# A mixture-of-experts layer's down product split in three, and ScalarE's order changed in the attention phases

## The chip, the core and the metric

The kernel runs on one core of a Trainium2 chip. The metric is the device time of one execution in microseconds (us). In the text PE is TensorE (its matmuls; PEld its weight loads), DVE is VectorE, ACT is ScalarE, POOL is GpSimd and SP is SyncE, which only issues DMAs here.

## The reference, cut to what matters

Sixteen sequences of 128 tokens with 128 features go through eight phases; each phase adds tanh(gate) times its result to x. Phases 0, 2, 4, 6 are attentions of different kinds, phases 1, 3, 5, 7 feed-forward layers. Phase 7 is the one that the change is mostly about, a mixture of 32 routed experts with hidden size 64, top 8 per token chosen within the best 4 of 8 groups, plus a shared expert of hidden size 128:

```
h    = layernorm(x)
s    = sigmoid(h @ router) (+ bias);  w = top-8 weights within the top 4 groups, normed, times 2.5
out  = sum_e w_e * ((silu(h @ Wg_e) * (h @ Wu_e)) @ Wd_e)  +  (silu(h @ Sg) * (h @ Su)) @ Sd
x    = x + tanh(g) * out
```

Every expert is computed for every token, and the weight w is zero for those not chosen.

## The kernel before

Tokens are held in four groups g of 512. A *step* is one group in one phase. Phase 0 comes first, then phases 1 and 3 (with phase 2 riding along) as `STREAMS[0]`, then phases 4 to 6 as *units* of attention heads (`heads_pe`, `heads_act`, `heads_dve`), then phase 7 as `STREAMS[1]`.

**A stream** (`stream_pe`, `stream_act`, `stream_pool`, `stream_dve`, lines 952 to 1282) goes through chunks n = 0, 1, ... In phase 7 each of the four groups has 17 chunks of 128 hidden rows (i = 0 is the shared expert, i = 1 to 16 routed ones), 68 in all. For one chunk:

- PE: the gate product into bank `B[n % 2]` and the up product into one of three banks, each as three fp32r matmuls of 128x512 (L870 to L872: high part of the weights by the low and the high part of x, low part of the weights by the high part of x). That is `product`.
- ACT: `sg = silu(gate)` (L1085), a ring of three.
- DVE: `hid = sg * up` (L1249), a ring of ten in SBUF.
- POOL, for i > 0: `hid *= bcs`, the token weights of this chunk's experts, spread over the partitions by DMA (L1213).
- PE, eight chunks later (`LAG`): the down product `Y += Wd * hid` as one fp32 matmul (L945, `stream_down`); a profile shows an fp32 matmul as two records.

Engines work in order, each through its own program. PE waits for `sg_ready` of chunk n-2 before a gate product, for `product_ready` of chunk n-3 before an up product, and for `weighted` before a down product. Hooks put steps of the next group at fixed chunks of the present one. In phase 7, for the next group: `xt` (transposes of its normed x, i = 1), `logits` (i = 4, in group 0 i = 6), `result` of the group before (i = 11), `turn` (i = 15, L969). `turn` transposes `comb`, the routing weights of the next group, waits for `comb_ready`, and stands in PE's program behind the products of chunk 15 and ahead of its down product. On ACT the sigmoid of the logits (`scores_act`, L905) comes one chunk after `logits` and needs another table: one table load before it and one before the next silu. On DVE the routing (`route_groups`) is a generator: from the chunk after `logits` on, one piece of it behind each product, seven pieces, the last one `comb` (L619). In group 0 these are chunks 7 to 13. The statistics of a later group (i = 10) and the update of x (L256, i = 11) stand among them. The transposed `comb` is copied to `w_row` by ACT (`turned_act`, chunk 16), stored and spread by SP's DMAs.

**The attention phases** work in units n of four heads by one sequence, 16 to a cycle c. PE's order in a unit: score(n), shift(n-1), the small steps of unit n (`compact_pe`, `rows`, `heads_turned_pe`, `result`, `values_pe`, `slots_pe`), turn(n-2), weigh(n-3). ACT's order in unit n: the small steps of unit n (L1470, L1361, L280, L287, and those of `slots_act`, L1957 and L1960 among them), exp of scores n (L1699), the copy `pt` of the transposed n-1 (L1709), the copy `os`. DVE takes the maxima (L1832) and its own small steps.

The lines quoted, from `stream_down`:

```python
nc.tensor.matmul(Y[:], w_raw[2][:, at:at + P], hid[(n0 + c) % HIDDEN],
                 start=(i == 0), stop=(i == m["NC"] - 1))
```

## Time and profile before

| what | value |
|---|---|
| median of 3 runs | 839.27 us (838.12 to 840.56) |
| the profiled execution | 840.37 us, span 838.6 us |
| phase 7 | about 670.9 us to the end |
| mean granted TensorE clock | 0.992 |

The span runs from the first to the last instruction; the execution's own time is 1.8 us longer. Rows give start, duration (us), engine, line, operation, output<-input, and in brackets the idle time of the engine before it with what ended it. Matmul records include their way through the array, so starts tell the spacing, not ends. The three matmul lines L870 to L872 are told from another by their tile names: gate or up.

### The profile page before, as it was taken

Reading aid. Unit: us, or ns where it says so; the run is one execution under the profiler, and the core shown is the slowest. Engines: PE = TensorE matmul, PEld = TensorE weight load, DVE = VectorE, ACT = ScalarE, POOL = GpSimd, SP = SyncE. Lnnn points to the kernel's source line nnn. Section 1 sums busy time; section 2 is a strip of 40 time slices with the busy share of each in tenths; the row PEclk is TensorE's granted clock in tenths of the full one; section 3 lists DMA queues with packets and bytes.
Section 4 is the critical chain, followed back from the end, with each engine's and each line's share of the span. In section 5 each row is a group of like instructions: output and inputs, shape, how many; then the busy total and the mean of one; then the engine's idle time right before and its main releaser. Section 6 shows DMA issues by size and latency. Waiting matters only on the chain.

```text
span 838.6 us, 13371 instructions
## 1 busy us (share of the span) xinstructions
PE 812.8 (97%) x4371; PEld 552.5 (66%) x4371; DVE 476.2 (57%) x1383; ACT 417.8 (50%) x762; POOL 446.2 (53%) x429
## 2 busy tenths in 40 slices
PE   4999999999999999999999999999999999999998
PEld 4876666777667666665666666656566576666664
DVE  6766536394846555335555757576755756545331
ACT  2434565656556343324666676756555562434221
POOL 5284655466654645376555444354545457565453
PEclk9799999999999999999999999999999999999999
DMA  9213030314423142441334131322213042424241
GB/s 317 83 50 102 1 101 1 100 65 159 134 70 100 53 145 57 139 123 41 80 95 114 42 98 44 97 49 54 64 41 90 28 150 69 148 71 145 70 154 46
DMA packets 44868, 75.27 MB, mean 90 GB/s; under 512 B 8992, under 2 KB 9632, under 8 KB 44672
## 3 DMA queue, kind: packets, MB, share of 16 engines
q1 hardware_dynamic: 44656, 74.42, 29.8%
q8 instruction: 35, 0.57, 0.3%
q14 instruction: 33, 0.27, 0.1%
q10 hardware_dynamic: 144, 0.01, 0.0%
HBM read 56.11 MB, written 1.51 MB: 69 GB/s over the span
## 4 chain that ended last, share of the span: by engine, by line
PE 87%; DVE 7%; ACT 2%; issue 2%; DMA 1%; SPq 0%; ACTq 0%; DVEq 0%
PE Y L945 21%; PE B L870 11%; PE B L872 11%; PE B L871 11%; PE B L1552 5%; PE B L1571 3%; PE B L1533 3%; PE B L1539 3%; PE B L1532 2%; PE T L1351 2%; DVE mxh L1832 2%; PE T L962 1%; DVE xhat L1815 1%; DMA CT<-in_ctx_t 1%; PE Y L1475 1%
## 5 line engine op out<-in xcount | busy, mean ns | idle before, releaser
L1213 POOL TENSOR_TENSOR shared<-shared,bcs 128x512 f32<-128x512 f32 x192 | 247.7, 1295 | 213.8 <-DVE shared L1249 189.4
L1249 DVE TENSOR_TENSOR shared<-shared,B 128x512 f32<-128x512 f32 x204 | 139.9, 687 | 222.5 <-PE B L872 182.9
L1085 ACT ACTIVATE shared<-B 128x512 f32<-128x512 f32 x204 | 121.7, 598 | 251.7 <-PE B L872 250.9
L945 PE MATMUL Y<-shared,down_lo 128*128 128x512 f32 x408 | 207.5, 594 | 0.0
L1772 POOL TENSOR_TENSOR shared_r<-shared_r,const 128x512 fp32r<-128x512 f32 (+1 forms) x128 | 115.6, 933 | 79.5 <-PE B L1533 37.4
L1832 DVE TENSOR_REDUCE mxh<-B 128x4 fp32r<-128x512 f32 (+1 forms) x128 | 78.7, 618 | 83.8 <-PE B L1533 82.7
L1709 ACT COPY shared<-B 128x512 f32<-128x512 f32 (+1 forms) x128 | 64.6, 505 | 59.8 <-PE B L1552 59.8
L1699 ACT ACTIVATE shared<-B 128x512 f32<-128x512 f32 (+1 forms) x128 | 69.4, 543 | 49.4 <-PE B L1539 47.9
L945 PEld LDWEIGHTS Y<-shared,down_lo 128*128 128x128 f32 x408 | 72.5, 190 | 21.4 <-issue 9.5
L870 PE MATMUL B<-shared_r,gate_hi 128*128 128x512 f32 x102 | 81.0, 795 | 0.0
L870 PE MATMUL B<-x_lo_r,gate_hi 128*128 128x512 f32 x102 | 75.7, 742 | 0.0
L1552 PE MATMUL B<-const,shared 128*128 128x128 f32 x448 | 71.9, 277 | 0.2 <-ACT shared L1709 0.2
L1552 PEld LDWEIGHTS B<-const,shared 128*128 128x128 f32 x448 | 53.6, 142 | 23.0 <-issue 14.2
L1533 PE MATMUL B<-shared_r 128*128 128x512 f32 (+1 forms) x128 | 67.2, 525 | 1.1 <-ACT shared L1699 1.1
L1539 PE MATMUL B<-mxh,minus_r 128*128 128x512 f32 (+1 forms) x128 | 48.3, 377 | 4.4 <-DVE mxh L1832 4.1
L1571 PE MATMUL B<-shared,vh 128*32 128x128 f32 x768 | 40.9, 285 | 0.0
L871 PE MATMUL B<-x_hi_r,gate_hi 128*128 128x512 f32 x102 | 40.6, 398 | 0.0
L872 PE MATMUL B<-shared_r,up_lo_r 128*128 128x512 f32 x102 | 40.5, 397 | 0.0
L872 PE MATMUL B<-x_hi_r,up_lo_r 128*128 128x512 f32 x102 | 40.4, 396 | 0.0
L872 PE MATMUL B<-x_hi_r,gate_lo_r 128*128 128x512 f32 x102 | 40.3, 395 | 0.0
L871 PE MATMUL B<-x_hi_r,up_hi 128*128 128x512 f32 x102 | 40.3, 395 | 0.0
L870 PE MATMUL B<-x_lo_r,up_hi 128*128 128x512 f32 x102 | 40.2, 394 | 0.0
(317 smaller groups left out, 1398.2 us busy)
## 6 DMA issues: line engine op xcount, KB each, us to landing
bcs<-wrow SPq DMA_DIRECT2D x96, 256.0 KB, 3.7
shared_r<-shared_r SPq DMA_DIRECT2D x256, 64.0 KB, 2.0
bcs<-wrow SPq DMA_DIRECT2D x128, 128.0 KB, 3.0
gate_lo<-in_moe SPq DMA_DIRECT2D x9, 256.0 KB, 5.3
up_lo<-in_moe SPq DMA_DIRECT2D x9, 256.0 KB, 6.0
down_lo<-in_moe SPq DMA_DIRECT2D x9, 256.0 KB, 3.7
small<-in_small SPq DMA_DIRECT2D x1, 1372.5 KB, 12.0
X<-in_x SPq DMA_DIRECT2D x4, 256.0 KB, 5.2
```

Of the source, the lines that this page charges most:

```text
L870: nc.tensor.matmul(out, w_hi[w][:, cols], lo, start=start, stop=False)
L871: nc.tensor.matmul(out, w_hi[w][:, cols], hi, start=False, stop=False)
L872: return nc.tensor.matmul(out, w_lo[w][:, cols], hi, start=False, stop=stop)
L945: nc.tensor.matmul(Y[:], w_raw[2][:, at:at + P], hid[(n0 + c) % HIDDEN], start=(i == 0), stop=(i == m["NC"] - 1))\
L1085: nc.scalar.activation(sg[(n0 + n) % ACTIVE], B[n % GATES][:], ACT.Silu).then_inc(sem("sg_ready"), 1)
L1213: gp.tensor_tensor(hid[(n0 + n) % HIDDEN], hid[(n0 + n) % HIDDEN], bcs[(PLACE.k0[p] + r // m["PER"]) % BROADCAST], ALU.mult)\
L1249: nc.vector.tensor_tensor(hid[(n0 + n) % HIDDEN], sg[(n0 + n) % ACTIVE], up[:], ALU.mult)\
L1533: mm(out, qh[a][:, cols], k_each[a % 2][:, :, cols], start=(p == 6), stop=True)\
L1539: mm(SC[u % 2][0:w, 0:4 * w].rearrange("p (i k) -> p i k", i=HEAD_TILES), minus_r[0:w, 0:w], mxh[u % 2][0:w, :].unsqueeze(2).to_broadcast( ...
L1552: ins = nc.tensor.transpose(PT[:, c], es[u % 2][:, c], ident)
L1772: ins = nc.gpsimd.tensor_tensor(k_each[a % 2][:, i, cols], kh[a % 2][:, cols].bitcast(F32), K("rowmask")[:, i:i + 1].to_broadcast([P, TG * ...
L1832: v.tensor_reduce(mxh[n % 2][0:w, :], SC[n % 2][0:w, 0:4 * w].rearrange("p (i k) -> p i k", i=4), AX.X, ALU.max).then_inc(sem("max_ready"), 1)
```

## The change

Chunks i = 5 to 16 of every group of phase 7 (`split`, 48 of them) get their down product as three fp32r matmuls instead of one fp32: high weights by low hid, high weights by high hid, low weights by high hid. For that:

- the down weights of these 12 chunks are split once: ACT copies the high part (`down_hi`) at chunks 3, 5, 7, four chunks of weights each, POOL subtracts for the low part at chunks 5, 7, 9;
- in a split chunk POOL multiplies `sg` by `bcs` ahead of DVE's product; DVE writes sg * up back into the up bank (PSUM); ACT copies it to `hid_hi` (`high`, in iteration n+1, after silu of n+1); DVE subtracts for the low part into `hid_low` (`low`, in iteration n+1, ahead of the product of n+1);
- phase 7's stream has four up banks instead of three, and the up product of chunk n+4 waits for `low` of n;
- the result copy of the group before moves from ahead of silu of chunk 8 to behind silu of chunk 7.

In `heads_act` the small steps of unit n+1 are issued between exp of n and the copy `pt` of n-1. Before, they came behind that copy. Of the `slots_act` steps only those at t = 1, 2 and 14 move, the others stay ahead of exp.

```diff
+WHOLE, HIGHS = 5, 10
+late = Area()
+down_hi = late.at_tile(15, [P, (MOE[7]["NC"] - WHOLE) * P], shared_r)
+hid_hi = [late.at_tile(18 + i, [P, TG], shared_r) for i in range(HIGHS)]
+def down_piece(q):
+    a, b = PIECES[7][q]
+    return slice((a - WHOLE) * P, (b - WHOLE) * P)
...
 bcs = [sb(f"bcs{i}", [P, TG])[:] for i in range(BROADCAST)]
+hid_at = area1.at
 hid = [area1.tile([P, TG]) for i in range(HIDDEN)]
+hid_low = [shared_r[:, hid_at + i * TG:hid_at + (i + 1) * TG] for i in range(HIDDEN)]
...
         self.n0 = PLACE.n0[phases[0]]
+        self.ups = UPS if ride else UPS + 1
+        self.split = {}
+        for n, (G, i) in enumerate(self.chunks):
+            p, g = self.groups[G]
+            if p == 7 and i >= WHOLE:
+                self.split[n] = len(self.split) + 1
...
+    def upper(self, n):
+        return B[GATES + n % self.ups]
...
             pe.wait_ge(sem(f"raw_down3_{q}"), 16)
+    if c in run.split:
+        for q, (a, _) in enumerate(PIECES[p]):
+            if (g, i) == (0, a):
+                pe.wait_ge(sem("down_lo_ready"), q)
+        at, w = i * P, (i - WHOLE) * P
+        hi, lo = hid_hi[run.split[c] % HIGHS], hid_low[(n0 + c) % HIDDEN]
+        pe.wait_ge(sem("hid_lo_ready"), run.split[c])
+        nc.tensor.matmul(Y[:], down_hi[:, w:w + P], lo, start=False, stop=False)
+        nc.tensor.matmul(Y[:], down_hi[:, w:w + P], hi, start=False, stop=False)
+        nc.tensor.matmul(Y[:], w_lo[2][:, at:at + P], hi, start=False, stop=(i == m["NC"] - 1))\
+            .then_inc(sem("down_mm") if i < m["NC"] - 1 else sem("y_ready"), 1)
+        return
...
                 .then_inc(sem("gated_mm"), 1)
-            if n >= UPS:
-                pe.wait_ge(sem("product_ready"), n0 + n - UPS + 1)
+            if n - run.ups in run.split:
+                pe.wait_ge(sem("hid_lo_ready"), run.split[n - run.ups])
+            elif n >= run.ups:
+                pe.wait_ge(sem("product_ready"), n0 + n - run.ups + 1)
...
                 pe.wait_ge(sem("p0_updated"), 2)
-            product(B[GATES + n % UPS][:], 1, slice(at, at + P), x_hi[g % 2], x_lo[g % 2])\
+            product(run.upper(n)[:], 1, slice(at, at + P), x_hi[g % 2], x_lo[g % 2])\
...
+    def high(n):
+        act.wait_ge(sem("product_ready"), n0 + n + 1)
+        k = run.split[n]
+        if k > HIGHS:
+            freed = next(c for c in run.split if run.split[c] == k - HIGHS)
+            H, i = run.chunks[freed]
+            after_down(act, *run.groups[H], i)
+        nc.scalar.copy(hid_hi[k % HIGHS], run.upper(n)[:]).then_inc(sem("hid_hi_ready"), 1)
...
         p, g = run.groups[G]
-        if i == LAG and G > 0:
+        if i == LAG and G > 0 and n - 2 not in run.split:
...
         nc.scalar.activation(sg[(n0 + n) % ACTIVE], B[n % GATES][:], ACT.Silu).then_inc(sem("sg_ready"), 1)
+        if G > 0 and i == LAG - 1 and n - 1 in run.split:
+            result_act(act, run.groups[G - 1][0], run.step(G) - 1)
+        if n - 1 in run.split:
+            high(n - 1)
+        if p == 7 and n in DOWN_ACT:
+            q = DOWN_ACT[n]
+            act.wait_ge(sem(f"raw1_{q}"), 96)
+            nc.scalar.copy(down_hi[:, down_piece(q)], w_raw[2][:, piece(7, q)])\
+                .then_inc(sem("down_hi_ready"), 1)
...
             weights_hi(act, 3, *SPLIT_ACT[n])
+    if len(run.chunks) - 1 in run.split:
+        high(len(run.chunks) - 1)
...
 SPLIT_ACT = {57: (0, 0), 58: (0, 1), 62: (1, 0), 63: (1, 1), 66: (2, 0), 67: (2, 1), 69: (3, 0), 70: (3, 1)}
+DOWN_ACT = {3: 1, 5: 2, 7: 3}
+DOWN_POOL = {5: 1, 7: 2, 9: 3}
...
             pool.wait_ge(loaded, count)
-            pool.wait_ge(sem("product_ready"), n0 + n + 1)
-            gp.tensor_tensor(hid[(n0 + n) % HIDDEN], hid[(n0 + n) % HIDDEN],
+            if n in run.split:
+                pool.wait_ge(sem("sg_ready"), n0 + n + 1)
+                by_weight = sg[(n0 + n) % ACTIVE]
+            else:
+                pool.wait_ge(sem("product_ready"), n0 + n + 1)
+                by_weight = hid[(n0 + n) % HIDDEN]
+            gp.tensor_tensor(by_weight, by_weight,
...
                 .then_inc(sem("weighted"), 1)
+        if p == 7 and n in DOWN_POOL:
+            q = DOWN_POOL[n]
+            c = piece(7, q)
+            pool.wait_ge(sem("down_hi_ready"), q)
+            gp.tensor_tensor(w_lo[2][:, c], w_raw[2][:, c], down_hi[:, down_piece(q)].bitcast(F32),
+                             ALU.subtract).then_inc(sem("down_lo_ready"), 1)
...
+    def low(n):
+        dve.wait_ge(sem("hid_hi_ready"), run.split[n])
+        if n >= HIDDEN:
+            H, i = run.chunks[n - HIDDEN]
+            after_down(dve, *run.groups[H], i)
+        nc.vector.tensor_tensor(hid_low[(n0 + n) % HIDDEN], run.upper(n)[:],
+                                hid_hi[run.split[n] % HIGHS].bitcast(F32), ALU.subtract)\
+            .then_inc(sem("hid_lo_ready"), 1)
...
             st.restart()
-        dve.wait_ge(sem("sg_ready"), n0 + n + 1)
-        dve.wait_ge(sem("upper_mm"), n0 + n + 1)
-        up = B[GATES + n % UPS]
-        if n >= HIDDEN:
-            before = run.chunks[n - HIDDEN]
-            after_down(dve, *run.groups[before[0]], before[1])
-        nc.vector.tensor_tensor(hid[(n0 + n) % HIDDEN], sg[(n0 + n) % ACTIVE], up[:], ALU.mult)\
-            .then_inc(sem("product_ready"), 1)
+        if n - 1 in run.split:
+            low(n - 1)
+        up = run.upper(n)
+        if n in run.split:
+            dve.wait_ge(sem("weighted"), PLACE.r0[p] + g * MOE[p]["NR"] + i - MOE[p]["SHARED"] + 1)
+            dve.wait_ge(sem("upper_mm"), n0 + n + 1)
+            nc.vector.tensor_tensor(up[:], sg[(n0 + n) % ACTIVE], up[:], ALU.mult)\
+                .then_inc(sem("product_ready"), 1)
+        else:
+            dve.wait_ge(sem("sg_ready"), n0 + n + 1)
+            dve.wait_ge(sem("upper_mm"), n0 + n + 1)
+            if n >= HIDDEN:
+                before = run.chunks[n - HIDDEN]
+                after_down(dve, *run.groups[before[0]], before[1])
+            nc.vector.tensor_tensor(hid[(n0 + n) % HIDDEN], sg[(n0 + n) % ACTIVE], up[:], ALU.mult)\
+                .then_inc(sem("product_ready"), 1)
...
             norm_stats(st, (run.step(H) + 2) % NG, run is STREAMS[0])
+    if len(run.chunks) - 1 in run.split:
+        low(len(run.chunks) - 1)
...
+OF_PE = (1, 2, 14)
 def heads_act(act):
-    for n in range(ALL + 3):
+    def step(n):
...
                 result_act(act, group(c - 1)[0], S4 + c - 1)
+            if t in OF_PE:
+                slots_act(act, c, t)
+    for n in range(ALL + 3):
+        c, t = divmod(n, NU)
+        if c < CYCLES and t not in OF_PE:
...
                                  scale=SCALEH).then_inc(sem("heads_es_ready"), 1)
+        step(n + 1)
```

## Rows read from the trace of the kernel before

**Rows 1.** The page, busy time, share of the span and instructions of each engine.

```profile
PE 812.8 (97%) x4371; PEld 552.5 (66%) x4371; DVE 476.2 (57%) x1383; ACT 417.8 (50%) x762; POOL 446.2 (53%) x429
```

**Rows 2.** The page, the chain that ended last, by line.

```profile
PE Y L945 21%; PE B L870 11%; PE B L872 11%; PE B L871 11%; PE B L1552 5%; PE B L1571 3%; PE B L1533 3%; PE B L1539 3%; PE B L1532 2%; PE T L1351 2%; DVE mxh L1832 2%; PE T L962 1%; DVE xhat L1815 1%; DMA CT<-in_ctx_t 1%; PE Y L1475 1%
```

**Rows 3.** The timeline of PE in group 0 of phase 7.

```profile
674.69 0.39 PE L871 MATMUL B<-x_hi_r,gate_hi 128*128 128x512 f32 x1
676.09 0.39 PE L871 MATMUL B<-x_hi_r,gate_hi 128*128 128x512 f32 x1
...
690.84 0.39 PE L871 MATMUL B<-x_hi_r,gate_hi 128*128 128x512 f32 x1
...
700.31 0.39 PE L871 MATMUL B<-x_hi_r,gate_hi 128*128 128x512 f32 x1
702.57 0.39 PE L871 MATMUL B<-x_hi_r,gate_hi 128*128 128x512 f32 x1
...
703.73 0.60 PE L969 MATMUL T<-const,comb 128*32 128x128 f32 x4
```

**Rows 4.** The timeline of ACT, chunks 7 and 8.

```profile
685.58 0.60 ACT L1085 ACTIVATE shared<-B 128x512 f32<-128x512 f32 x1 [1.03 <-PE B L872]
686.19 1.28 ACT L905 ACT_TABLE_LOAD   x1
...
687.78 1.28 ACT L1085 ACT_TABLE_LOAD   x1
689.08 1.09 ACT L1085 ACTIVATE shared<-B 128x512 f32<-128x512 f32 x2
```

**Rows 5.** The timeline of DVE, routing in group 0, and L688 of group 1.

```profile
689.76 0.69 DVE L1249 TENSOR_TENSOR shared<-shared,B 128x512 f32<-128x512 f32 x1 [0.20 <-ACT shared L1085]
690.36 0.38 DVE L593 MAX8 m<-gv 128x8 f32<-128x12 f32 x4
...
698.73 1.31 DVE L688 SCALAR_TENSOR_TENSOR w<-work,sig 128x128 f32<-128x128 f32 x1
...
701.42 0.28 DVE L619 SCALAR_TENSOR_TENSOR comb<-w,rec 128x128 f32<-128x128 f32 x1
...
734.22 0.90 DVE L688 SCALAR_TENSOR_TENSOR w<-work,sig 128x128 f32<-128x128 f32 x1
```

**Rows 6.** Busy us of PE, PEld, DVE, ACT, POOL; then clock, DMA share, GB/s.

```profile
689.76:701.70 11.94, 11.94 (x46) 8.11 (x45) 11.46 (x48) 3.40 (x6) 8.19 (x8) 1.00 0.30 89
```

**Rows 7.** Groups of instructions: xcount, busy us, mean ns, idle before.

```profile
L1268 DVE TENSOR_TENSOR shared_r<-T,shared_r 128x512 fp32r<-128x512 f32 x1 | 0.7, 691 | 0.1
L1103 ACT CAST shared_r<-T 128x512 fp32r<-128x512 f32 x6 | 3.6, 606 | 0.0
L1213 POOL TENSOR_TENSOR shared<-shared,bcs 128x512 f32<-128x512 f32 x192 | 247.7, 1295 | 213.8 <-DVE shared L1249 189.4 <-DMA bcs<-wrow 24.0
L2026 DVE TENSOR_TENSOR B<-B,m 128x256 f32<-128x256 f32 x4 | 1.7, 432 | 0.1
L2001 DVE TENSOR_TENSOR x_lo<-x_lo,B 128x256 f32<-128x256 f32 x4 | 1.7, 420 | 0.1
```

**Rows 8.** The timeline of POOL beside L688.

```profile
698.61 1.28 POOL L1213 TENSOR_TENSOR shared<-shared,bcs 128x512 f32<-128x512 f32 x1
```

**Rows 9.** Busy time in two stretches, columns as in rows 6 (PE, PEld, DVE, ACT, POOL, clock).

```profile
637.75:641.16 3.41, 2.06 (x15) 1.21 (x14) 2.73 (x4) 1.05 (x4) 3.41 (x4) 1.00 0.41 101
641.16:644.58 3.42, 3.42 (x15) 2.48 (x14) 1.03 (x2) 1.97 (x4) 0.31 (x1) 0.50 0.43 101
```

**Rows 10.** The timeline of DVE and PE in group 1: comb and turn.

```profile
737.93 0.28 DVE L619 SCALAR_TENSOR_TENSOR comb<-w,rec 128x128 f32<-128x128 f32 x1
744.15 0.60 PE L969 MATMUL T<-const,comb 128*32 128x128 f32 x4
```

**Rows 11.** Waits in the attention phases: waiting<-waited for, total us, times, longest.

```profile
PE B L1926 <- ACT bcs L1960: 0.4, 2, 0.3
PEld B L1926 <- ACT bcs L1960: 2.2, 4, 0.7
```

## The prediction

> **What bounds the kernel now.** I read the page first: TensorE (PE) is busy in 97% of the span, DVE in 57%, ACT in 50%, POOL in 53% [rows 1], and the chain that ended last lies mostly on PE, 21% of it on the down product, L945 [rows 2]. So I then read PE's own timeline in phase 7. A chunk without a down product takes 676.09 - 674.69 = 1.40 us from one L871 to the next; it is six fp32r matmuls, so 0.234 us each. A chunk with its fp32 down product takes 702.57 - 700.31 = 2.26 us [rows 3]. The fp32 product thus costs 0.86 us of PE. From chunk 8 on no PE row of phase 7 shows a wait: the stage is PE's issue time and nothing else. Last I read ACT and DVE in the same stretch, for how late they may become before PE waits [rows 4 to 6], and the list of waits in the attention phases for the reorder.
>
> **1. The split down product.** Removed: 48 fp32 products (4 groups, 12 of 17 chunks) at 0.86 us. Added: 3 fp32r matmuls each, of the form of L870 to L872, 3 x 0.234 = 0.70 us. PE saves 0.16 us per chunk at most; over all chunks the period with a down product is nearer to 2.25, so I take 0.15: 48 x 0.15 = 7.2 us (7.7 at 0.16). All of it is on the path, since PE is. The last eight down products are among the 48.
> The Trainium skill (TensorE: Matmul & The Clock Gate, Back-to-back issue gap) has N/2.4 + 2.5 ns, 216 ns for 512 columns; by that three products would cost 0.65 us and the split would save 10.3 us instead. The trace spaces these very matmuls at 0.234 us, so it disagrees, and the row is what I use.
>
> **2. What the split puts on the other engines.** Per split chunk, DVE gets the subtraction `low` (the form of L1268, 0.69 us; what follows such an op starts 0.60 after it, 690.36 behind 689.76), ACT gets the copy `high` (L1103, 0.61 us), POOL's multiplication stays at 1.29 us but is now ahead of DVE's product instead of behind it [rows 5, 7]. The product is now written to PSUM; for 128x256 the writes to PSUM (L2026, 0.432) and to SBUF (L2001, 0.420) cost the same [rows 7], so nothing is added. The way of one chunk becomes silu, weight, product, high, low: 0.60 + 1.29 + 0.69 + 0.61 + 0.69 = 3.9 us, about 4.4 with five hand-overs of 0.1 (silu's end at 689.68 to the product at 689.76 is 0.08 [rows 4, 5]). Down products come eight chunks later, and behind the very last chunk seven other down products and its own up product still cover 8 x 0.70 = 5.6 us, so the tail is not lengthened. The four up banks leave about 4 us of lateness: up product n+4 is wanted 4 x 2.1 = 8.4 us after n's gate, `low` of n is nominally done 4.2 us after it. On average all is covered: DVE adds 48 x 0.60 = 29 us and ACT about as much to engines half idle. It is not covered where routing stands.
>
> **3. ACT at chunk 7.** Before: silu of 7 at 685.58, sigmoid table 686.19, silu table 687.78, silu of 8 at 689.08 [rows 4]. In that same iteration ACT now also issues `high` of 6 and the last copy of down weights, 0.49 to 0.61 each: silu of 8 starts at 690.2 and ends at 690.8. PE wants its bank for chunk 10 at about 690.4 (its second matmul, L871, was at 690.84 [rows 3]). PE waits some 0.4 us; between 0 and 1. The other two weight copies (ACT, chunks 3 and 5) and the three subtractions on POOL (1.3 us each, chunks 5, 7, 9) are nominally within idle time: ACT is idle over 1 us per chunk, and POOL 0.9. If that cover were gone they would add to this same wait.
>
> **4. DVE's routing in group 0.** This is the step that decides. PE's `turn` for group 1 stands after chunk 15, at 703.73 [rows 3], and waits for comb. All later matmuls of PE are queued behind it. In the trace comb ends at 701.42 + 0.28 = 701.70 [rows 5], 2.0 us early. From the product of chunk 8 (689.76) to there DVE is busy 11.46 of 11.94 us [rows 6], with six products and routing, statistics and the update between them; the rest is starts. After: the product of 8 waits for silu (690.8), for POOL's 1.29 and two hand-overs: 692.4. Five `low` (8 to 12) go between, 5 x 0.60 = 3.0. Comb ends at 692.4 + 11.9 + 3.0 = 707.3. PE arrives two shortened down products earlier (-0.3) but 0.4 later by part 3: 703.8. So PE waits 3.5 us, 3.6 with the hand-over. Bounds: 2.5 (L688 at 0.90 as in group 1 instead of 1.31 [rows 5], and the product of 8 some 0.6 sooner) and 5 (0.69 for each `low` and product, and 0.5 of waiting for `high`).
> L688, one of the routing instructions, took 1.31 us here, with POOL's L1213 at work from 698.61 [rows 5, 8], and 0.90 in group 1; I keep 1.31. The Trainium skill (SBUF — State Buffer, Who interferes with whom) says that a DVE instruction with two SBUF inputs and a GpSimd instruction that reads SBUF block each other; L688 fits that, `low` and product have one PSUM input each and would stay at 0.69, and were the block gone by the new order the sum would be 0.4 us less.
>
> **5. The clock.** In the attention stage, from 637.75 to 641.16, PE was busy 2.06 of 3.41 us, so idle for 1.35; in the next stretch, 3.42 us, the granted clock was 0.50, the 1.2 GHz level [rows 9]. A full stop of 3.6 us at `turn` is longer than that one, and the matmuls before and behind it are the dense kind, which speaks a little against it. At half the clock 3.4 us yield the work of 1.7 us: a cost of 1.7, or 0. I take 1.7.
> That idle time lets the granted clock fall is also in the Trainium skill (TensorE: Matmul & The Clock Gate, Part 1); the trace agrees with its level.
>
> **6. Groups 1 and 2.** There routing begins two chunks earlier. In group 1 comb starts at 737.93 and `turn` at 744.15 [rows 10]: 6 us early. Seven `low` take 4.2, POOL's place ahead of the product up to 1.4 at the start, PE's own gain over ten chunks up to 1.0 the other way. Between 0 and 2 us remain, so I take no wait; group 3 routes nothing. Later there: w_row is copied on ACT behind `high`, one or two us later, so the first multiplications of a group begin later on POOL; its chunks 1 to 4 are not split and their down products are eight chunks away.
>
> **7. ACT's order in the attention phases.** Nothing is added. The small steps that PE issues ahead of the transposes of a unit (compact, rows, heads turned, result, three of the slot steps) are now taken by ACT in that order, not behind the copy of the unit before. Each is ready 0.5 to 1 us sooner; the transposed copy may come later but has a whole unit till it is used. What can be won are PE's waits for such steps: at L1926, the largest of them, the array was idle for 0.4 us and the weight load for 2.2 [rows 11]. The first is a floor, since much of a weight load's wait lies under the matmul before it, the second a ceiling. The other steps wait less, so I stay between: -1.2. Bound on the other side: +0.5, from the last cycle's short units, where a copy of 0.6 comes ahead of a pt copy.
>
> **The sum**, against the profiled execution (840.37 us, span 838.6 and 1.8 around it): -7.2 + 0.4 + 3.6 + 1.7 - 1.2 = -2.7, or 837.7. It was 1.1 above the median of the runs, 839.27; on that the forecast is 836.6 us.
>
> **Rivals.**
> *The wait at `turn` stays away or is small* (DVE absorbs `low`; product of 8 early). For: over the whole span DVE is busy 57% only. Against: the 11.94 us without idle time. Then -7.2 - 1.2 = 830.9. Chance 0.12.
> *The wait comes, the clock holds.* For: PE stood dense before and after. Then 836.6 - 1.7 = 834.9. Chance 0.25.
> *The forecast, wait and clock:* 836.6. Chance 0.40, half of it below and half above 836.75.
> *A longer wait, 5 to 6 us, with the clock:* 838 to 839. Chance 0.13.
> *Slower: DVE late at all three turns.* If x us more are lost between routing's start and comb in each group (two-input routing ops at 1.31 like L688, `low` waiting for ACT), the waits are 3.6 + x, x - 1 and x - 2 and two more clock falls at 1.7 follow. At x = 3 that is 3 x 3 + 0.6 = 9.6 and 5.1 for clocks, less 8.4 and with 0.4 from part 3: +6.7, 846. It turns slower than before at x = 2 (5.6 + 1.0 of waits, one or two falls at 1.7, against 8.0). For: DVE is full in that stretch. Against: the routing starts two chunks earlier there. Chance 0.10.
>
> **How the numbers follow.** A measurement tells 0.3%, 2.5 us, from no change, so the border is 836.75. Faster: 0.12 + 0.25 + about 0.15 = 0.52. Same: the rest of the forecast and 0.13, 0.38. Slower by over 2.5 us: 0.10. The range, 831.5 to 840.5, leaves out the last case and most of the first; its lower end is the saving nearly whole, its upper end is the longer wait with the reorder worth nothing.
>
> **What would show it.** Right: 144 fp32r matmuls at 0.23 us in phase 7 and chunks with them 2.10 us apart; one PE wait of 3 to 4 us ahead of the transposes of comb after chunk 15, released by DVE L619, none at the later two; a stretch at half clock behind it; DVE without idle time from the product of chunk 8 to comb. Wrong: no PE wait there (then 831), PE waiting for `low` ahead of an up product (banks too few), or split chunks over 2.2 us apart. In the attention phases, the wait before L1926 gone and no new one before L1571.

## The result and the profile after

The changed kernel takes 835.35 us (median of 4 runs, 833.73 to 835.43) against 839.91 us (4 runs, 838.12 to 840.56) of the kernel before, run beside it: ratio 0.9944, interval 0.9924 to 0.9965. The forecast was 836.6 us with a range of 831.5 to 840.5. The profiled execution after took 833.73 us, with a span of 831.9. It was the fastest of the four; the other three took 835.3 to 835.4 us at a mean granted clock of 0.989, against 0.993 here, so they spent more time at the lower clock. In the start-up of the kernel, ahead of all that was changed, it is 1.1 us ahead of the profiled execution before. The clock goes with that: from about 20 us on it was at the 1.2 GHz level for 10.2 us before and for 3.4 us after.

The page of the kernel after, first the engines, then the chain by line, then groups of instructions (busy us, mean ns | idle before, and its releaser):

```profile
PE 802.1 (96%) x4419; PEld 559.9 (67%) x4419; DVE 503.6 (61%) x1431; ACT 445.6 (54%) x813; POOL 450.6 (54%) x432
...
PE Y L979 15%; PE B L892 10%; PE B L894 10%; PE B L893 10%; PE B L1641 5%; PE B L1660 4%; PE B L1622 3%; PE B L1628 3%; PE B L1621 2%; DVE mxh L1930 2%; PE T L1440 2%; PE Y L971 1%; PE Y L969 1%; PE Y L970 1%; DVE xhat L1913 1%
...
L1314 DVE TENSOR_TENSOR shared_r<-B,shared_r 128x512 fp32r<-128x512 f32 x48 | 33.2, 692 | 23.2 <-ACT shared_r L1121 19.3
L1121 ACT CAST shared_r<-B 128x512 fp32r<-128x512 f32 x48 | 28.1, 586 | 35.4 <-DVE B L1328 34.9
```

Against [rows 1] PE is busy 10.7 us less and DVE 27.4 us more, and PE still bounds: the fp32 down product (L979, L945 before) fell from 21% to 15% of the chain, the three new matmuls (L969 to L971) took 1% each. There are 48 `high` (L1121) and 48 `low` (L1314), at 0.59 and 0.69 us, near the lengths that step 2 took for them.

Now PE's timeline in phase 7 of the kernel after (start, duration; in brackets the idle time just before). Its matmuls L892 to L894 are L870 to L872 of [rows 3]:

```profile
669.30 0.41 PE L893 MATMUL B<-x_hi_r,gate_hi 128*128 128x512 f32 x1
...
686.63 0.40 PE L893 MATMUL B<-x_hi_r,gate_hi 128*128 128x512 f32 x1
...
689.29 0.50 PE L892 MATMUL B<-x_lo_r,gate_hi 128*128 128x512 f32 x1 [0.47 <-ACT shared L1130]
689.62 0.40 PE L893 MATMUL B<-x_hi_r,gate_hi 128*128 128x512 f32 x1
...
696.85 0.39 PE L893 MATMUL B<-x_hi_r,gate_hi 128*128 128x512 f32 x1
...
698.95 0.39 PE L893 MATMUL B<-x_hi_r,gate_hi 128*128 128x512 f32 x1
...
701.05 0.39 PE L893 MATMUL B<-x_hi_r,gate_hi 128*128 128x512 f32 x1
...
704.66 0.60 PE L1003 MATMUL T<-const,comb 128*32 128x128 f32 x4 [2.28 <-DVE comb L631]
706.02 0.40 PE L893 MATMUL B<-x_hi_r,gate_hi 128*128 128x512 f32 x1
...
819.92 0.39 PE L893 MATMUL B<-shared_r,gate_hi 128*128 128x512 f32 x1
```

Three readings. Two chunks with a split down product stand 698.95 - 696.85 = 2.10 us apart, where they stood 2.26 apart [rows 3]. At chunk 10 PE stood 0.47 us for ACT's silu, and the step from chunk 9 to 10 took 689.62 - 686.63 = 2.99 us. And at `turn` after chunk 15 the array stood 2.28 us for comb, so that 701.05 to 706.02 is 4.97 us. The same step takes 2.53 us at the `turn` of groups 1 and 2 of this kernel, and took 2.70 us in group 0 of the kernel before. From the first to the last of these matmuls phase 7 takes 819.92 - 669.30 = 150.6 us. In the kernel before it was this:

```profile
671.24 0.39 PE L871 MATMUL B<-x_hi_r,gate_hi 128*128 128x512 f32 x1
...
825.14 0.39 PE L871 MATMUL B<-shared_r,gate_hi 128*128 128x512 f32 x1
```

153.9 us: 3.3 less now. Behind the last of them the execution has 11.95 us left, 13.45 before: the last eight down products, 1.5 less. So phase 7 gives 4.8 us net. With what the two waits cost added (2.44 us at `turn`; 0.73 at chunk 10) it is 8.0 us gross, or 0.166 us for each of 48 products.

The wait and the stretch behind it in the kernel after (busy us of PE, PEld, DVE, ACT, POOL; then the granted clock, the DMA share, GB/s):

```profile
702.38:704.66 2.28, 0.00 (x0) 0.03 (x1) 2.03 (x6) 0.34 (x2) 2.28 (x3) 1.00 0.00 0
704.66:711.00 6.34, 6.34 (x30) 5.20 (x31) 4.08 (x7) 4.12 (x9) 3.68 (x4) 1.00 0.06 13
```

PE did nothing for 2.28 us, and the granted clock stayed at 2.4 GHz behind it. The clock fall that the forecast counted didn't come in this execution.

The whole difference of the two profiled executions, 840.37 - 833.73 = 6.6 us, is then 1.1 in the start-up, 0.9 in the attention phases (290.3 to 289.4 us, with one more clock fall of 3.4 us there than before), 3.3 in the chunks and 1.5 in the tail, 0.2 more than the total by rounding and ends.

### The profile page after: what moved, and what is told of

It reads as the page before. It is cut to its first block, busy times and chain, and to the rows that moved or that the text cites. A ratio compares the mean times of both kernels' runs of the same rounds, so it can differ in the third digit from the quotient of the medians.

```text
span 831.9 us, 13639 instructions
## 1 busy us (share of the span) xinstructions
PE 802.1 (96%) x4419; PEld 559.9 (67%) x4419; DVE 503.6 (61%) x1431; ACT 445.6 (54%) x813; POOL 450.6 (54%) x432
## 4 chain that ended last, share of the span: by engine, by line
PE 83%; DVE 9%; ACT 3%; issue 2%; POOL 1%; DMA 1%; SPq 0%; DVEq 0%; ACTq 0%; POOLq 0%
PE Y L979 15%; PE B L892 10%; PE B L894 10%; PE B L893 10%; PE B L1641 5%; PE B L1660 4%; PE B L1622 3%; PE B L1628 3%; PE B L1621 2%; DVE mxh L1930 2%; PE T L1440 2%; PE Y L971 1%; PE Y L969 1%; PE Y L970 1%; DVE xhat L1913 1%
## 5 line engine op out<-in xcount | busy, mean ns | idle before, releaser
L1336 DVE TENSOR_TENSOR shared<-shared,B 128x512 f32<-128x512 f32 x156 | 106.5, 686 | 160.1 <-PE B L894 120.0
L979 PE MATMUL Y<-shared,down_lo 128*128 128x512 f32 x312 | 159.7, 595 | 0.0
L892 PE MATMUL B<-shared_r,gate_hi 128*128 128x512 f32 x102 | 71.5, 701 | 0.0
L892 PE MATMUL B<-x_lo_r,gate_hi 128*128 128x512 f32 x102 | 69.2, 679 | 0.9 <-ACT shared L1130 0.9
L979 PEld LDWEIGHTS Y<-shared,down_lo 128*128 128x128 f32 x312 | 54.9, 190 | 14.6 <-issue 5.9
L1314 DVE TENSOR_TENSOR shared_r<-B,shared_r 128x512 fp32r<-128x512 f32 x48 | 33.2, 692 | 23.2 <-ACT shared_r L1121 19.3
L1121 ACT CAST shared_r<-B 128x512 fp32r<-128x512 f32 x48 | 28.1, 586 | 35.4 <-DVE B L1328 34.9
L1328 DVE TENSOR_TENSOR B<-shared,B 128x512 f32<-128x512 f32 x48 | 33.1, 689 | 14.6 <-POOL shared L1276 14.4
L894 PE MATMUL B<-x_hi_r,up_lo_r 128*128 128x512 f32 x102 | 40.4, 396 | 0.0
L894 PE MATMUL B<-x_hi_r,gate_lo_r 128*128 128x512 f32 x102 | 40.3, 395 | 0.0
```

The lines of the kernel that those rows point to most:

```text
L892: nc.tensor.matmul(out, w_hi[w][:, cols], lo, start=start, stop=False)
L894: return nc.tensor.matmul(out, w_lo[w][:, cols], hi, start=False, stop=stop)
L1336: nc.vector.tensor_tensor(hid[(n0 + n) % HIDDEN], sg[(n0 + n) % ACTIVE], up[:], ALU.mult)\
```

## The experiments

Two things are read from each kernel: the time, as a ratio to the kernel before on the same chip, and two stretches of its profile, "the attention stretch" (first score matmul to the first L871 of phase 7; 290.3 us before, 289.4 after) and "the chunks of phase 7" (first L871 to last; 153.9 and 150.6). Medians of two measurements of one and the same kernel differ by some 3 us (the repeat below), so stretches decide more than times do.

**The reorder alone.** The kernel before with ACT's new order in the attention phases and nothing else; the change below without it comes next.

```diff
+        OF_PE = (1, 2, 14)
...
-            for n in range(ALL + 3):
+            def step(n):
...
+                    if t in OF_PE:
+                        slots_act(act, c, t)
+            for n in range(ALL + 3):
+                c, t = divmod(n, NU)
+                if c < CYCLES and t not in OF_PE:
...
+                step(n + 1)
```

> The kernel before with ACT's new order in the attention phases alone. My account: PE's waits for ACT's small steps go (before L1926 above all) and the attention phases end 1 to 2 us sooner against their own start; phase 7 stays at 153.9 us from its first to its last chunk. Time 1 to 2 us under the kernel before. Rival (the order matters little, the whole gain is the split's): within 0.5 us of the kernel before. Second rival (the earlier end of a step moves DVE's long instructions onto each other, as in the longer wait of 2.4 us at 635 us of the changed kernel): the same wait of over 2 us shows here, and the gain is under 1 us.

Measured: 837.44 us (12 runs) against 840.61, ratio 0.9963 (0.9947 to 0.9979), 3.1 us. The attention stretch is 288.6 us, the chunks of phase 7 are 153.88, unchanged. One clock fall in the stretch lasted 6.8 us here and 3.4 before:

```profile
635.50:642.30 6.80, 6.60 (x29) 4.50 (x29) 2.73 (x5) 3.42 (x8) 1.73 (x2) 0.50 0.41 100
```

At half the clock 6.6 us of PE's work cost 3.3 more; the fall of 3.4 us before cost 1.7. Without either the stretch is 288.6 - 3.3 = 285.3 against 290.3 - 1.7 = 288.6: the order is worth 3.3 us there, where 1 to 2 were expected. The wait of over 2 us for `mxh`, the second rival's sign, doesn't show in this kernel (1.4 us).

**The split alone.** The changed kernel with the loop of the kernel before in `heads_act`.

> The changed kernel with ACT's old order in the attention phases: the split alone. My account: PE saves 48 x 0.166 = 8.0 us, and gives back 2.4 at the turn of group 0 and 0.7 at the gate product of chunk 10; phase 7 ends 4.8 us sooner against its start, and 1.7 less where the granted clock falls behind the turn. Time 3 to 5 us under the kernel before. Rival (the reorder sets when phase 7's inputs come and the waits are its doing): the waits at turn and gate are under half of that.

Measured: 836.62 us (12 runs), ratio 0.9957 (0.9939 to 0.9975). The attention stretch is 293.8, with 10.2 us at half clock in it: 293.8 - 5.1 = 288.7, that of the kernel before. So the two parts stand apart. The chunks of phase 7 take 152.2. The wait at `turn` is that of the changed kernel, 2.3 us for comb, but behind it this execution has the fall that the forecast had counted, for 3.4 us (windows of this kernel, columns as above):

```profile
706.90:710.30 3.40, 1.39 (x9) 1.20 (x10) 2.90 (x7) 1.09 (x2) 2.85 (x4) 1.00 0.00 0
710.30:713.70 3.40, 3.40 (x10) 2.63 (x9) 2.09 (x4) 2.24 (x4) 2.86 (x3) 0.50 0.03 5
```

3.40 us of matmuls at the 1.2 GHz level would cost 1.7 us by half the speed; the chunks are 152.2 - 150.6 = 1.6 us longer than in the changed kernel, whose steps are otherwise the same. The same stop of 2.3 us was followed by a fall here and by none in the changed kernel.

**Group 0 left whole.** Groups 1 to 3 are split, group 0 is not, and the parts of the weights are made later.

```diff
+        SPLIT_FROM = {0: 17, 1: 5, 2: 5, 3: 5}
...
-                    if p == 7 and i >= WHOLE:
+                    if p == 7 and i >= SPLIT_FROM[g]:
...
-        DOWN_ACT = {3: 1, 5: 2, 7: 3}
-        DOWN_POOL = {5: 1, 7: 2, 9: 3}
+        DOWN_ACT = {16: 1, 17: 2, 18: 3}
+        DOWN_POOL = {18: 1, 22: 2, 26: 3}
```

> The changed kernel with group 0 not split (12 fp32 products come back, +2.0 us) and the down weights split later, ACT in chunks 16 to 18, POOL in 18, 22 and 26. If the five low of chunks 8 to 12 and the copies at chunk 7 are what makes PE wait, the wait at turn (2.4) and at chunk 10's gate (0.7) are gone, comb ends about 2 us before turn, and the time is 0.8 to 1.2 us under the changed kernel, 2 to 3 us where its clock falls behind the turn. Rival (comb is late for another reason, POOL's order or the earlier start of the stage): the wait at turn stays over 1 us, and the time is 1 to 2 us above the changed kernel.

Measured: 831.24 us (4 runs), ratio 0.9886 (0.9866 to 0.9906). The chunks of phase 7 take 149.3 us, 1.3 less than with group 0 split, though twelve fewer products are split. No wait of PE at chunk 10 or at `turn` is left, and no clock fall among the chunks. The accounts agree: 36 x 0.166 = 6.0 us, against 153.9 - 149.3 = 4.6 and 1.5 in the tail. No execution of the changed kernel stands in this measurement, so the expected difference of 0.8 to 1.2 us in time isn't tested by it; the stretch bears it out.

**A later last piece.** The changed kernel with the last copy of down weights on ACT at chunk 10 instead of 7, and POOL's subtraction at 12 instead of 9.

```diff
-        DOWN_ACT = {3: 1, 5: 2, 7: 3}
-        DOWN_POOL = {5: 1, 7: 2, 9: 3}
+        DOWN_ACT = {3: 1, 5: 2, 10: 3}
+        DOWN_POOL = {5: 1, 7: 2, 12: 3}
```

> The changed kernel with the last piece of down weights copied by ACT at chunk 10 instead of 7 and subtracted by POOL at chunk 12 instead of 9. My account: ACT's table loads at chunk 7 start 0.5 us sooner, so the product of chunk 8 too; PE's wait for chunk 10's gate falls from 0.7 to 0.2, that at turn from 2.4 to about 2.1 (DVE's chain starts 0.5 sooner, the PE arrives 0.5 sooner too: then 2.4 stays and only the first is won). Time 0.5 us under the changed kernel. Rival (the copy is hidden): no difference in either wait.

Measured: 835.21 us (6 runs), ratio 0.9942 (0.9923 to 0.9962). The first half came as expected: from chunk 9 to 10 it is 2.48 us instead of 3.0, so the copy of a piece is what makes silu late there. The second half didn't: comb became later, not earlier.

```profile
PE T L1007 <- DVE comb L635: 3.8, 1, 3.8
```

With the longer wait a fall of 6.8 us came behind it (5.02 us of PE's work in it, so some 2.5 us lost), and the chunks of phase 7 took 153.9. Where the time went is in DVE's timeline of this kernel. The first line is the product of chunk 8, the others are routing:

```profile
688.32 0.70 DVE L1334 TENSOR_TENSOR B<-shared,B 128x512 f32<-128x512 f32 x1 [0.20 <-POOL shared L1280]
...
693.04 1.20 DVE L700 TENSOR_TENSOR vals<-s,gm 128x128 f32<-128x128 f32 x1
...
700.71 0.80 DVE L630 TENSOR_SCALAR tot<-tot 128x4 f32<-128x4 f32 x1
...
702.95 0.68 DVE L635 SCALAR_TENSOR_TENSOR comb<-w,rec 128x128 f32<-128x128 f32 x1
```

and POOL's timeline of the same kernel:

```profile
692.81 1.28 POOL L1280 TENSOR_TENSOR shared<-shared,bcs 128x512 f32<-128x512 f32 x1 [1.25 <-ACT shared L1134]
...
702.22 1.26 POOL L1280 TENSOR_TENSOR shared<-shared,bcs 128x512 f32<-128x512 f32 x1
```

L700 is what L684 was before (0.28 us there), L635 what L619 was (0.28). They ended 0.15 us behind POOL's multiplication: 693.04 + 1.20 = 694.24 against 692.81 + 1.28 = 694.09, and 702.95 + 0.68 = 703.63 against 702.22 + 1.26 = 703.48. L630, 0.17 us in the kernel before (L614), ran from 700.71 to 701.51, and POOL's multiplication between these two, of 1.33 us from 700.14, to 701.47. From the product of chunk 8 to the end of comb this kernel took 15.31 us, the changed kernel 13.81. Four routing instructions make the whole difference to the changed kernel: L700 0.73 longer, L630 0.63, L635 0.38, and L683, the L667 of the kernel before, 0.22 shorter. Moving two instructions of POOL and ACT changed which routing instructions fall on one of POOL's.

**The changed kernel again,** on the chip of the three that follow, with no edit.

> The changed kernel once more, beside the others of this call. My account, from the first four runs: wait at turn 2.4, at chunk 10's gate 0.7; behind the turn the granted clock falls in most executions, for 3.4 us or twice that, so the median lies 4 to 5 us under the kernel before. Rival (no fall behind the turn, as in the first profile): 6 us under it.

Measured: 832.03 us (6 runs) against 841.04 (17 runs), ratio 0.9899 (0.9875 to 0.9924). The median is 9.0 us under the kernel before, more than the account (4 to 5) and the rival (6) had. The chunks of phase 7 are 150.62, the wait at `turn` 2.3 and no fall behind it, all as in the first profile. The attention stretch is 287.4 us, 2.0 less than there: 1.2 of it lies in the sixteen score matmuls that had the additional clock fall, 0.8 in the last sixteen, where PE waits 1.4 us for `mxh` and not 2.4. The intervals of the two ratios just touch at 0.9924. Within each measurement the time goes with the clock: three of the first four executions have a mean granted clock of 0.989, five of these six have 0.992 to 0.996, and the sixth, at 0.988, is the slowest (836.35 us). At the same 0.993 the first measurement has 833.73 and this one 830.54 and 831.44, so the clock isn't all of the difference; the rest stays open.

**Every `low` of group 0 twice.** One more subtraction of the same form on DVE ahead of the real one, into a tile that nobody reads.

```diff
...
+                if run.chunks[n][0] == 0:
+                    nc.vector.tensor_tensor(low_again, run.upper(n)[:],
+                                            hid_hi[run.split[n] % HIGHS].bitcast(F32), ALU.subtract)
```

> The changed kernel with each low of group 0 issued twice on DVE (the first into a scratch tile): 5 more of them between the product of chunk 8 and comb, two earlier. If DVE's chain is what PE waits for at turn, comb comes 5 x 0.6 = 3.0 us later and the wait grows from 2.4 to 5.2 to 5.6; the time grows by 3 us, and by up to 1.7 for a surer or longer fall of the clock. Rival (POOL's weighting or ACT's high sets comb's time, and DVE has slack between): the wait grows by under 1.5 us.

Measured: 838.64 us (10 runs), ratio 0.9975 (0.9959 to 0.9990); 6.6 us above the changed kernel, where 3 to 4.7 were expected. PE's waits in this kernel:

```profile
PE T L1004 <- DVE comb L632: 4.6, 1, 4.6
...
PE B L893 <- DVE shared_r L1318: 0.8, 2, 0.4
```

Comb ended 3.97 us later after the start of the stage (39.18 us against 35.21): the five copies in the chain and one ahead of the product of chunk 8 make 3.6 of it. DVE has no slack here, what is added ahead of comb arrives at comb. PE's wait grew by 2.3, between the account's 2.8 to 3.2 and the rival's 1.5; PE was itself late by then, by the 0.8 of the second line, a wait for `low` ahead of up products, among others. Behind `turn` came a fall of 6.8 us. With it the chunks of phase 7 took 157.1 us, more than before the change.

**Group 0 split for its last four chunks only.** The `low` of chunks 13 to 16 stand behind comb in DVE's program. The edit is shown against the kernel with the later last piece.

```diff
-        SPLIT_FROM = {0: 5, 1: 5, 2: 5, 3: 5}
+        SPLIT_FROM = {0: 13, 1: 5, 2: 5, 3: 5}
...
-        DOWN_ACT = {3: 1, 5: 2, 10: 3}
-        DOWN_POOL = {5: 1, 7: 2, 12: 3}
+        DOWN_ACT = {14: 3, 17: 1, 18: 2}
+        DOWN_POOL = {16: 3, 18: 1, 22: 2}
```

> Group 0 split in chunks 13 to 16 only, behind the last piece of routing, later groups from chunk 5 on as in the changed kernel. No low stands ahead of comb then, and 40 products are split against 36 of the run without group 0. My account: no wait at turn or gate, no clock fall there, 4 x 0.166 = 0.7 us under that run's 831.2, or 830.5. Rival (any split in group 0 costs its gain again, since ACT's copy at chunk 14 and POOL's subtraction at 16 meet the last pieces): equal to or above 831.2.

Measured: 830.09 us (5 runs), ratio 0.9868 (0.9847 to 0.9889), the lowest time of the study. The chunks of phase 7 take 814.56 - 665.80 = 148.8 us:

```profile
665.80 0.41 PE L897 MATMUL B<-x_hi_r,gate_hi 128*128 128x512 f32 x1
...
814.56 0.39 PE L897 MATMUL B<-shared_r,gate_hi 128*128 128x512 f32 x1
```

Of phase 7's waits on PE none is above 0.7 us (its last turned result), none stands at chunk 10 or at `turn`, and no clock fall stands among the chunks. 40 x 0.166 = 6.6 us, and 153.9 - 148.8 + 1.5 = 6.6. Its ratio and that of the kernel with group 0 whole overlap (0.9866 to 0.9906), so the two are told apart by the stretch, 0.5 us, and not by the time.

**Two more chunks of groups 1 to 3.** The kernel above with those groups split from chunk 3 on; the weights' part for chunks 3 and 4 is made at chunks 15 (ACT) and 17 (POOL).

```diff
-        SPLIT_FROM = {0: 13, 1: 5, 2: 5, 3: 5}
+        SPLIT_FROM = {0: 13, 1: 3, 2: 3, 3: 3}
...
-        DOWN_ACT = {14: 3, 17: 1, 18: 2}
-        DOWN_POOL = {16: 3, 18: 1, 22: 2}
+        DOWN_ACT = {14: 3, 15: 0, 17: 1, 18: 2}
+        DOWN_POOL = {16: 3, 17: 0, 18: 1, 22: 2}
```

> As the run before it, and chunks 3 and 4 of groups 1 to 3 split too: 46 products. My account: 6 x 0.166 = 1.0 us less, if POOL has caught up with the late token weights of a group's first chunks by chunk 3. Rival: it has not (its multiplication of chunk 1 waits 3.3 us for the DMA in the kernel before), DVE's product of chunk 3 waits for it, PE waits for an up bank, and the time is 1 to 4 us above the run before it.

Measured: 833.3 us (6 runs), ratio 0.991 (0.9889 to 0.993). Six more products split made the chunks of phase 7 151.9 us, 3.2 longer. One line of DVE's waits in this kernel, and the longest of PE among the chunks:

```profile
DVE B L1339 <- POOL shared L1285: 16.0, 6, 6.1
...
PE B L901 <- ACT shared L1139: 1.0, 1, 1.0
PE Y L988 <- ACT ysb L287: 0.8, 1, 0.8
PE B L901 <- DVE shared_r L1325: 0.6, 1, 0.6
```

Against the kernel above, chunk by chunk, PE loses 0.3 and 0.8 us at chunks 8 and 15 of group 1, 1.5 at chunks 7 and 8 of group 2 and 1.3 at chunks 6 and 8 of group 3. The rival named the start of this: DVE's product of chunk 3, the first split one, waits 3.7, 4.5 and 6.1 us for POOL's multiplication in the three groups, and POOL's first multiplication of the group had waited 4.0, 5.5 and 6.0 us for the DMA of the token weights. That these waits and PE's later ones are one chain is argued from their order, not shown by a run.

**`turn` one chunk later.** The changed kernel with the transposes of comb for group 1 after chunk 16.

```diff
-                        table.update(xt=1, logits=6)
+                        table.update(xt=1, logits=6, turn=NC - 1)
```

> The changed kernel with the turn of group 0 one chunk later on PE, behind chunk 16 instead of 15; nothing is taken from DVE. If PE's wait is only that comb comes 2.4 us behind PE's arrival, one chunk of products, 2.1 us, now fills it: the wait falls from 2.4 to 0.3, the granted clock does not fall there, and phase 7's chunks take 148.5 us instead of 150.6. Price: ACT copies w_row a chunk later, PE waits for that copy ahead of the transposes of the group after next's x (chunk 18), at most 1 us. Rival (the lost time moves to that wait): phase 7 as long as in the changed kernel.

Measured: 832.8 us (6 runs) against 841.02, ratio 0.9906 (0.9878 to 0.9934). The wait for comb is gone, and the chunks of phase 7 are 150.62 us, not one tenth shorter. PE's waits:

```profile
PE T L1009 <- ACT w_row L940: 1.9, 1, 1.9
PE B L892 <- ACT shared L1130: 0.5, 1, 0.5
```

The wait has moved one link down: the copy of the turned weights on ACT is now late for PE's next use of that bank, at chunk 18 (4.60 us there instead of 2.52).

**Less of POOL's work.** The kernel with the later last piece, with POOL's multiplication in chunks 8 to 13 of group 0 cut to 8 of 512 columns; most of those chunks stays unweighted, all else is as it was.

```diff
+                    cols = slice(0, 8) if p == 7 and 8 <= n <= 13 else slice(0, TG)
-                    gp.tensor_tensor(by_weight, by_weight,
+                    gp.tensor_tensor(by_weight[:, cols], by_weight[:, cols],
...
```

> The kernel of e4 with POOL's token weighting of chunks 8 to 13 of group 0 cut to 8 of 512 columns (the rest of these chunks stays unweighted). In e4 DVE took 15.3 us from the product of chunk 8 to comb's end, in the changed kernel 13.8, with the same instructions; both hold routing instructions that last longer than elsewhere (1.20 for vals against 0.28, 0.80 for tot against 0.17) while a POOL instruction runs. If POOL's reads are what holds them, the 15.3 falls to 13.2 to 13.5, vals is at 0.28 to 0.30, tot at 0.17, and the wait at turn to under 1 us (comb also 1.1 us sooner, since the product of 8 no longer waits for a weighting of 1.29). Rival (they are long for another reason, the rate of instruction issue or ACT): vals and tot keep their lengths and the stretch takes over 14.5 us.

Measured, one execution: 836.45 us against 839.78; the wait at `turn` 2.6 us instead of 3.8, where under 1 was expected. DVE's timeline of this kernel:

```profile
690.58 0.69 DVE L1321 TENSOR_TENSOR shared_r<-B,shared_r 128x512 fp32r<-128x512 f32 x1 [1.22 <-ACT shared_r L1125]
691.19 0.69 DVE L1335 TENSOR_TENSOR B<-shared,B 128x512 f32<-128x512 f32 x1
...
695.90 0.28 DVE L700 TENSOR_TENSOR vals<-s,gm 128x128 f32<-128x128 f32 x1
...
702.65 1.25 DVE L630 TENSOR_SCALAR tot<-tot 128x4 f32<-128x4 f32 x1
```

L700 is back at 0.28 us, with no multiplication of POOL beside it. L630, on 128x4 elements, took 0.80 before and takes 1.25 now, and this is what POOL did then, the first multiplication that was not cut:

```profile
702.61 1.27 POOL L1281 TENSOR_TENSOR shared<-shared,bcs 128x512 f32<-128x512 f32 x1 [0.63 <-ACT shared L1134]
```

702.65 to 703.90 beside 702.61 to 703.88: DVE's instruction ended when POOL's did. This is the strongest sign of the hold between the two engines; the wait became shorter because fewer such meetings were left. The product of chunk 8 came only 0.3 us sooner (the first line says why: the `low` of chunk 7 ahead of it waited 1.22 us for ACT's `high`), so nearly all of the gain lies behind it, in a chain of 14.45 us instead of 15.31. Three instructions make it up: L700 0.92 shorter, L635 0.40 shorter (0.68 to 0.28), L630 0.45 longer. The chain was expected at 13.2 to 13.5, with L630 at 0.17; that it met a full multiplication again is the difference.

## Why the prediction was right, and where it was off

The time lies 1.25 us under the forecast and under 836.75, the border that the forecast drew for faster. The mechanism was right, a saving on PE of which comb at `turn` takes part back. The nearness of the number is partly luck: all of the five terms below but that of chunk 10 were set too high, the found ones add up to 3.8 to 5.4 us less than the forecast's -2.7, and the repeat of the kernel, 832.03 us, lies only just inside the range. By term, forecast against found:

| term | forecast, us | found, us | from |
|---|---|---|---|
| split, step 1 | -7.2 | -8.0 | chunks and tail of phase 7 |
| ACT at chunk 10, step 3 | +0.4 | +0.7 | step from chunk 9 to 10 |
| comb at `turn`, step 4 | +3.6 | +2.4 | step over `turn` |
| clock, step 5 | +1.7 | 0 or +1.6 | changed kernel; split alone |
| reorder, step 7 | -1.2 | -3.2 | stretch, time of the reorder alone |

The sum of the found terms is -8.1 without a fall and -6.5 with one. The first measurement has -4.6 at the medians and the repeat -9.0, so the sum lies between the two, and their spread is larger than any single term's miss.

**Step 1** had its mechanism and its rate right. I had taken 0.15 instead of the 0.16 of the two periods because "over all chunks the period with a down product is nearer to 2.25"; the split period turned out at 2.08 to 2.10 as well, so the difference was 0.16 to 0.17 over all 48. The rule of the Trainium skill weighed there (TensorE: Matmul & The Clock Gate, Back-to-back issue gap), which the page gives for an isolated matmul, would have given some 10 us; the stretches of three kernels with 36, 40 and 48 split products give 0.165 to 0.17 each, so by the rows and not by the rule. That no PE row from chunk 8 on shows a wait was read wrongly: the kernel before has one of 0.7 us, ahead of its last turned result, and the changed kernel has the same, so it cost the sum nothing.

**Step 2** held: nothing on ACT, DVE or POOL reaches PE from it outside routing and the one silu. The tail got shorter by 1.5 us, that is 8 x 0.166 = 1.3 and a little.

**Step 3** had the place and the cause right. The timeline of ACT in the kernel after shows the sequence that was forecast behind the silu of 7: `high` of 6, the copy of the piece, the table, and at the end the silu of 8:

```profile
684.63 0.59 ACT L1121 CAST shared_r<-B 128x512 fp32r<-128x512 f32 x1 [0.40 <-DVE B L1328]
685.11 0.62 ACT L1138 CAST shared_r<-down_lo 128x512 fp32r<-128x512 f32 x1
685.75 1.28 ACT L927 ACT_TABLE_LOAD   x1
...
688.64 0.60 ACT L1130 ACTIVATE shared<-B 128x512 f32<-128x512 f32 x1
```

What was left out is the bracket of 0.40: `high` of 6 waits for the product of 6. With the copy of the piece taken away the cost fell from 0.7 to 0.2 us.

**Step 4** decided, as it said. PE waited once, at the `turn` it named, for comb, and at neither of the later two. The wait was 2.3 us and not 3.6, under the lower bound of 2.5. The start of its chain was right: the product of chunk 8 began at 690.71, which is 690.71 - 669.30 + 671.24 = 692.65 in the frame of the kernel before, where 692.4 was forecast. What failed is the length of the chain, 13.81 us instead of 11.94 + 3.0. PE also came to `turn` 0.3 us later than forecast, by what step 3 cost more, and that shortens its wait. DVE's timeline of the kernel after:

```profile
690.71 0.70 DVE L1328 TENSOR_TENSOR B<-shared,B 128x512 f32<-128x512 f32 x1 [0.20 <-POOL shared L1276]
692.13 0.69 DVE L1314 TENSOR_TENSOR shared_r<-B,shared_r 128x512 fp32r<-128x512 f32 x1 [0.23 <-ACT shared_r L1121]
...
694.01 0.40 DVE L679 TENSOR_SCALAR gm<-gwork 128x32 f32<-128x32 f32 x1
...
695.65 0.47 DVE L696 TENSOR_TENSOR vals<-s,gm 128x128 f32<-128x128 f32 x1
...
701.95 0.29 DVE L700 SCALAR_TENSOR_TENSOR w<-work,sig 128x128 f32<-128x128 f32 x1
...
704.21 0.30 DVE L631 SCALAR_TENSOR_TENSOR comb<-w,rec 128x128 f32<-128x128 f32 x1
```

and one of the same routing instructions in the kernel before:

```profile
692.28 0.87 DVE L667 TENSOR_SCALAR gm<-gwork 128x32 f32<-128x32 f32 x1
```

L700 here is L688 of [rows 5], at 0.29 us instead of 1.31: the step said "I keep 1.31". L679 (L667 before) took 0.40 instead of 0.87, and L696 (L684) 0.47 instead of 0.28. Together 1.3 us shorter; one wait of 0.23 for `high` goes the other way. The rule weighed in that step (SBUF — State Buffer, Who interferes with whom, of the Trainium skill) has a DVE instruction with two SBUF inputs contend with a GpSimd instruction that reads SBUF. In the kernel after, L700 starts where POOL's multiplication ends,

```profile
700.78 1.30 POOL L1276 TENSOR_TENSOR shared<-shared,bcs 128x512 f32<-128x512 f32 x1
```

0.13 us before its end, and is short; the trace agrees with the rule, and two experiments moved the meetings about and saw the durations follow. What the step took as one instruction's property is a property of what POOL happens to do beside it. Not every instruction of POOL holds: comb, at 704.21 above, runs beside POOL's L1256, a TENSOR_SCALAR from 704.12 to 705.01, and takes 0.30. The estimate there, "0.4 us less", was short by 0.6, since it counted from L688 of group 1, 0.90, which was partly held too: it ended at 735.12, 0.16 behind a multiplication of POOL.

The price of the wait is shown from two sides. Without the `low` in front of comb (group 0 whole, or its last four chunks) it is gone and the chunks are 1.3 to 1.9 us shorter with fewer products split; with twice the `low`, comb is 4 us later.

**Step 5** was right in its kind and undecided in its size. A fall of the granted clock behind the stop of PE at `turn` came in four of the profiled kernels: at stops of 2.3 (split alone), 2.6, 3.8 and 4.6 us; it lasted 3.4, 3.4, 6.8 and 6.8. It did not come in the changed kernel and in its repeat, with a stop of 2.3 us each. So the stops of 2.6, 3.8 and 4.6, each seen once, were followed by one, the stop of 2.3 in one execution of three. The attention phases show the same: all twelve profiles have a stop of PE of 1.6 us at about 455 us, and the clock fell behind it in two of them, the changed kernel's first and the split alone. In what the executions with and without differ stays open. The three executions of the first measurement without a profile had a mean clock of 0.989, against 0.993 of the profiled one; over 832 us that is some 7 us more at the 1.2 GHz level (an estimate), and whether it lay behind `turn` no trace shows.

**Step 6** held: no wait of PE at the `turn` of groups 1 and 2. Comb was 2.5 and 4.8 us early there, where between 0 and 2 were forecast.

**Step 7** was mis-sized most. It read one wait of the weight load, 2.2 us at L1926, took that as a ceiling and stayed under it. But the list of waits has more lines of the same kind:

```profile
PEld T L1351 <- ACT xhat_t L280: 1.4, 3, 0.5
PEld B L1915 <- ACT bcs L1957: 1.4, 3, 0.6
PEld T L1351 <- ACT shared L1470: 1.1, 2, 0.6
```

Together with the 2.2 of [rows 11] they are 6.1 us, and all are gone in the kernel with the reorder alone and in the changed kernel. One line grew in exchange: the weight loads of the transposes (L1552) wait 4.9 us for ACT's exp instead of 2.0. What is left, 6.1 - 2.9 = 3.2, is as much as was gained; that each us of these waits was worth one isn't shown. "The other steps wait less, so I stay between" priced them at nothing, as the ceiling of the whole was that of one of them. The gain is spread: of the attention phases' eight cycles of sixteen score matmuls the six in the middle became shorter, in the reorder alone and in the repeat of the changed kernel, by 0.4 to 0.7 us each, 3.2 in all. In the changed kernel's first profile 2.0 us of that are lost again, in the cycle with the additional clock fall (1.2) and in the last one (0.8), where PE waits 1.0 us more for the maximum `mxh` (longest wait 2.4, against 1.4 in the kernel before and in the repeat).

Of the rivals, the one in which the wait comes and the clock holds (834.9) is nearest to the time and describes both profiles of the changed kernel; for its other executions no trace tells. The one in which the wait stays away belongs to the kernels with group 0 mostly whole; the slower one, DVE late at all three turns, has nothing for it. The chances have a slip: half of the forecast's 0.40 was put below 836.75, but 0.15 of it was counted as faster, so faster should have been 0.57 and not 0.52.

## What to carry to other kernels

Work moved here from the bounding engine to a half idle one was paid back where that engine is full, however low its mean: the best version leaves eight products of group 0 as they were, since their extra work stands in front of a join, and is at 830.1 us where the changed kernel on the same chip is at 832.0. The intervals of these two ratios overlap, so it is the chunks of phase 7 that tell them apart, 148.8 against 150.6 us. Read all lines of a kind in the list of waits before you put a ceiling on a reorder. And ask of a long duration of a small instruction whether it is a meeting with another engine, which a shift of either can make or undo; here moving two instructions by three chunks cost 1.5 us of wait.

## What was not expected of the hardware

I had reckoned with held instructions of two SBUF inputs only. A DVE instruction on 128x4 elements with one tensor input (`tot`, a TENSOR_SCALAR, 0.17 us in the kernel before) took 0.80 and 1.25 us beside POOL's multiplication, and ended within 0.04 and 0.02 us of it. L667, another TENSOR_SCALAR, took 0.87 in the kernel before, 0.40 in the changed one and 0.18 in the one with the later last piece; the two long ones ended 0.04 us behind a multiplication of POOL (693.15 and 693.11, 694.41 and 694.37), and beside the short one POOL stood idle. The section of the Trainium skill on who interferes with whom does name tensor_scalar among the operations that can take the shared ports, in a mode that uses both; in which mode these ran no run here shows. And a stop of PE of 2.3 us was followed by a clock fall in one execution and by none in two others, with the same instructions on either side of it.
